# Attention and entropy layers on one core: next image's projection begins at the end of attention, in four PSUM banks, with three value banks ahead of the entropy steps

## The reference

```python
x = x + attention(_gn(x), w1, b1, a1, w2, b2, a2, wa, ba, aa)
#   q = prelu(w1 x + b1), k = prelu(w2 x + b2)   24 channels each
#   v = prelu(wa x + ba)                         192 channels
#   out = softmax(q^T k) v                       4096 x 4096 scores for each image
x = x + likelihood(_gn(x), m0..m3, b0..b3, f0..f2)
#   for lower = x - 0.5 and upper = x + 0.5, in each channel: four small layers 1 -> 3 -> 3 -> 3 -> 1,
#   logits = softplus(m) logits + b, and after the first three: logits += tanh(f) tanh(logits)
#   likelihood = max(|sigmoid(s upper) - sigmoid(s lower)|, 1e-6)
```

## Time and profile before

| | |
|---|---|
| median of 3 runs | 4902.97 us (4902.42 to 4907.78) |
| the profiled execution's own time | 4911.56 us |
| its span in the trace | 4909.8 us |
| busy: PE, DVE, ACT, POOL | 91%, 86%, 73%, 15% |

### The profile page before, as it was taken

The page is one execution under the profiler, slowest core; times in us unless marked ns, Lnnn a source line. Parts: engine busy times, 40 slices in busy tenths (PEclk is TensorE's granted clock), DMA queues, the critical chain, the costliest instruction groups (busy, mean ns, idle before and its releaser), DMA issues.

```text
span 4909.8 us, 106055 instructions
## 1 busy us (share of the span) xinstructions
PE 4460.9 (91%) x38328; PEld 2970.3 (60%) x38328; DVE 4209.1 (86%) x5569; ACT 3600.0 (73%) x3958; POOL 726.6 (15%) x769
## 2 busy tenths in 40 slices
PE   6999889998899988999899998999989998899976
PEld 4887338873488724787258862688616785178831
DVE  6997799978999789997899968999699996989866
ACT  2666887668767697676977669776697776966788
POOL 4200300003010130101300022000220103101012
PEclk9999999999999999999999999999999999999998
DMA  3001431014301142011520024210241113420133
GB/s 78 14 17 32 109 84 30 23 41 114 81 23 32 35 119 73 23 31 42 124 61 27 28 60 117 49 34 21 69 113 47 31 30 74 104 51 23 34 86 95
DMA packets 154987, 279.93 MB, mean 57 GB/s; under 512 B 37441, under 2 KB 37921, under 8 KB 152706
## 3 DMA queue, kind: packets, MB, share of 16 engines
q1 hardware_dynamic: 154434, 272.69, 21.6%
HBM read 205.24 MB, written 50.33 MB: 52 GB/s over the span
## 4 chain that ended last, share of the span: by engine, by line
PE 56%; DVE 16%; ACT 12%; issue 12%; DMA 1%; SPq 1%; DVEq 0%; POOL 0%; ACTq 0%; POOLq 0%
PE ps L1345 10%; PE ps L1347 10%; PE ps L1349 10%; PE ps L1121 7%; ACT th L669 6%; PE ps L1297 6%; DVE mxp L1026 5%; ACT arena L662 4%; DVE arena L922 3%; DVE th L960 3%; PE ps L1218 2%; PE ps L1204 2%; PE ps L1165 2%; PE ps L1176 2%; PE ps L1146 2%
## 5 line engine op out<-in xcount | busy, mean ns | idle before, releaser
L1345 PE MATMUL ps<-v_sb,arena 128*128 128x193 f16 x8192 | 2016.0, 246 | 14.7 <-DVE arena L922 14.7
L1347 PE MATMUL ps<-v_sb,arena 128*128 128x192 f16 x8192 | 2024.9, 247 | 0.0
L1349 PE MATMUL ps<-v_sb,arena 128*128 128x193 f16 x8192 | 2007.8, 245 | 0.0
L626 ACT ACTIVATE arena<-ps 128x1024 f16<-128x1024 f32 x1024 | 1050.5, 1026 | 896.3 <-PE ps L1121 896.2
L922 DVE TENSOR_TENSOR arena<-arena 128x1024 f16<-128x1024 f32 x1024 | 1293.6, 1264 | 213.7 <-ACT arena L629 213.6
L1026 DVE TENSOR_REDUCE mxp<-ps 128x1 f32<-128x512 f32 x1792 | 1177.9, 686 | 50.1 <-PE ps L1297 40.4
L960 DVE SCALAR_TENSOR_TENSOR th<-th,gates,ps 128x1024 f32<-128x1024 f32 x768 | 950.7, 1275 | 206.0 <-ACT th L669 201.0
L629 ACT ACTIVATE arena<-ps 128x1024 f32<-128x1024 f32 x1024 | 1045.6, 1021 | 0.2 <-DVE arena L922 0.2
L1347 PEld LDWEIGHTS ps<-v_sb,arena 128*128 128x128 f16 x8192 | 794.4, 97 | 262.4
L669 ACT ACTIVATE th<-ps,biases 128x1024 f32<-128x1024 f32 x768 | 827.0, 1118 | 114.1 <-PE ps L1204 77.8
L1345 PEld LDWEIGHTS ps<-v_sb,arena 128*128 128x128 f16 x8192 | 791.3, 97 | 143.6 <-issue 26.2
(11 more groups left out here) (120 smaller groups left out, 3189.7 us busy)
## 6 DMA issues: line engine op xcount, KB each, us to landing
x<-x2d SPq DMA_DIRECT2D x1152, 64.0 KB, 2.2
arena<-x2d SPq DMA_DIRECT2D x768, 64.0 KB, 2.4
xp<-x_dram SPq DMA_DIRECT2D x18, 1536.0 KB, 12.9
shared<-x_dram SPq DMA_DIRECT2D x64, 384.0 KB, 3.7
x2d<-shared SPq DMA_DIRECT2D x64, 384.0 KB, 3.0
res<-x2d SPq DMA_DIRECT2D x96, 256.0 KB
out_dram<-res SPq DMA_DIRECT2D x96, 256.0 KB
kst<-shared SPq DMA_DIRECT2D x32, 256.0 KB, 4.3
```

What stands on the lines that cost most here:

```text
L626: act.activation(e_hi[:, q % 4, :].rearrange("p (k n) -> p k n", k=2), sc, ACT.Exp)
L1345: pe.matmul(acc, eh, v_sb[:, m, 0:C + 1], start=(m == 0 and t % 2 == 0), stop=False, skip_group_check=True)
L1347: pe.matmul(acc[:, 0:C], eh, v_sb[:, m, VW:VW + C], start=False, stop=False, skip_group_check=True)
L1349: ins = pe.matmul(acc, el, v_sb[:, m, 0:C + 1], start=False, stop=(m == MT - 1), skip_group_check=True)
```

## The change

- `project(0)`, the next image's first query and key bank, moves on PE from the beginning of `phase_a` to the end of `phase_b`, behind the last block's matmuls. This is ahead of the loop's branch. Its ACT and DVE parts now come ahead of `add_half`, and `low_part(0)` moves behind the third piece of `chain2`.
- The query and key banks go round four PSUM banks (`n % 4`), and the waits of PE change with them (`bank_user`).
- `V_LEAD` falls from 6 to 3: the value banks in the entropy steps are in steps 0 to 12 in place of 0 to 9.
- The first maximum moves from step 11 to step 14 (`FIRST_AT`). Steps 14 to 38 hold 31 of them and step 39 the last: one in a step, two in steps 15, 19, 23, 27, 31 and 35. The split and the turn come one step earlier.

```diff
-V_LEAD = 6
+V_LEAD = 3
-FIRST_AT = 11
+FIRST_AT = VB - V_LEAD + 1
+TURN_AT = 43
+def first_maxima(s):
+    begin = sum(2 if k % 4 == 3 else 1 for k in range(FIRST_AT, s))
+    return list(range(begin, min(begin + (2 if s % 4 == 3 else 1), MAXES))) if s >= FIRST_AT else []
+def bank_of(n):
+    return n % 4 if n < QK else n % 2
+def bank_user(n):
+    return max(n - 3, 0) if n < QK + 2 else n - 1
...
 # POOL
                     queries(0)
+                    queries(1)
                 root2(l)
                 if proj:
-                    for n in range(1, QK):
+                    for n in range(2, QK):
...
 # DVE
                 denominators(l, BLOCKS - 1)
+                if proj:
+                    value(0)
                 add_half(l, BLOCKS - 1, 0)
                 add_half(l, BLOCKS - 1, 1)
...
                 next(chain2)
                 if proj:
-                    query(0)
-                next(chain2)
+                    value(1)
                 next(chain2)
                 next(chain2)
                 if proj:
-                    query(1)
+                    low_part(0)
+                next(chain2)
                 next(chain2)
...
-                        m = s - FIRST_AT
-                        if 0 <= m < MAXES:
+                        for m in first_maxima(s):
...
 # PE
+            def project(n):
+                for h in range(2):
+                    k = HALF + h
+                    ins = pe.matmul(ps[:, bank_of(n), :], w_s[0:k, h, 0:P], xp[0:k, h, n * N:(n + 1) * N],
+                                    start=(h == 0), stop=(h == 1))
+                ins.then_inc(proj_mm, 1)
...
                 def bank_free(n):
-                    if n >= 2:
-                        pe.wait_ge(val_ready, pj(BANKS, n - 1))
+                    if bank_user(n):
+                        pe.wait_ge(val_ready, pj(BANKS, bank_user(n)))
...
                 if proj:
-                    qk_bank(0)
                     qk_bank(1)
                 averages2(l, 0)
...
-                    if proj and 0 <= s - FIRST_AT < MAXES:
-                        first_max(s - FIRST_AT)
+                    if proj:
+                        for m in first_maxima(s):
+                            first_max(m)
...
 # PE, end of phase_b
+                pe.wait_ge(full_ready, pairs + PAIRS)
+                project(0)
```

More of the change, by code:

```diff
@@ L649, in negative @@
                         act.wait_ge(val_ready, pj(BANKS, n - 1))
-                    act.activation(p_neg[:, n % 2, 0:w], ps[:, n % 2, 0:w], ACT.Relu, scale=-1.0
+                    act.activation(p_neg[:, n % 2, 0:w], ps[:, bank_of(n), 0:w], ACT.Relu, scale=-1.0
                                    ).then_inc(neg_ready, 1)
@@ L936, in value @@
                     dve.scalar_tensor_tensor(p_val[:, n % 2, 0:w], p_neg[:, n % 2, 0:w], omac[:, col:col + 1],
-                                             ps[:, n % 2, 0:w], ALU.mult, ALU.add).then_inc(val_ready, 1)
+                                             ps[:, bank_of(n), 0:w], ALU.mult, ALU.add).then_inc(val_ready, 1)
                 def low_part(n):
@@ L1017, in phase_a @@
                                               ALU.max).then_inc(max_red, 1)
-                        if m == MAXES:
+                        if s == TURN_AT - 1:
                             split_max(pj(BLOCKS, 0), pj(BLOCKS * MAXES, 0))
-                        if m == MAXES + 1:
-                            rows_out(pj(BLOCKS, 0), 0, l is None)
+                        if s == TURN_AT:
+                            rows_out(pj(BLOCKS, 0), 0, False)
             def phase_b(b, l):
@@ L1159, in qk_bank @@
                         pe.wait_ge(ws_ready, pj(1, 1))
-                        if l is not None:
-                            pe.wait_ge(full_ready, l * BLOCKS * PAIRS + BLOCKS * PAIRS)
                     bank_free(n)
-                    for h in range(2):
-                        k = HALF + h
-                        ins = pe.matmul(ps[:, n % 2, :], w_s[0:k, h, 0:P], xp[0:k, h, n * N:(n + 1) * N],
-                                        start=(h == 0), stop=(h == 1))
-                    ins.then_inc(proj_mm, 1)
+                    project(n)
                 def value_bank(v):
@@ L1175, in value_bank @@
                             k = HALF + h
-                            ins = pe.matmul(ps[:, n % 2, i * C:(i + 1) * C], xp[0:k, h, m * P:(m + 1) * P],
+                            ins = pe.matmul(ps[:, bank_of(n), i * C:(i + 1) * C], xp[0:k, h, m * P:(m + 1) * P],
                                             w_s[0:k, h, P:PW], start=(h == 0), stop=(h == 1))
@@ L1282, in phase_a @@
                             second_layer(s - 1)
-                        if proj and s == FIRST_AT + MAXES + 1:
+                        if proj and s == TURN_AT:
                             turn_max(pj(BLOCKS, 0), 0)
```

## The result

The changed kernel took 5031.99 us in the median of 4 runs (5025.67 to 5040.27), against 4905.38 us (4902.42 to 4909.45) for the kernel before on the same chip: a ratio of 1.026 (95% interval 1.0248 to 1.0272). It is slower by 126.6 us, 18 us for each of the seven images whose `phase_a` carries the projection. The forecast was 4993 with a range up to 5022. The sign was right and so was the chain of waits behind the largest term; the time lies above the range.

The account below looks back on a forecast made before the run. PE, DVE and ACT are busy most of the time; ACT's chain through PE and DVE paces the entropy steps. Terms -6.2 + 1.2 + 2.3 + 16.2 - 0.6 = 12.9 us an image, 90 for seven: 4993 us, range 4922 to 5022.

Parts of the forecast that it names:

- The double steps: Steps with two maxima, 15 to 35: waits for DVE's reductions hold `second_layer` and delay ACT, +16.2 us an image.
- The change-over: From one image's attention to the next's first step: earlier norm and fewer value banks ahead, -6.2 us an image in sum.
- Bank 0 and the branch: At the loop's end, two matmuls queued ahead of PE's branch cost 0.3 us an image, bounds nothing to 1.7-2.7.
- The rival in which the bank delays the branch until both matmuls are through: At the loop's end, `turn_out` starts 1.7 us later in six images, 5001 us in all; chance 0.05.
- The first maximum: Step 14: the wait for the last value bank moves here from step 11 and delays ACT, +2.3 us an image.
- The moved value banks: Steps 10 to 12: ACT has one more `negative` in each, about 0.4 us apiece, +1.2 us an image.
- The end of the steps: Steps 40 to 42: no maximum on PE any more where ACT waits for PE, -0.6 us an image.
- faster: Entropy steps: the maxima's waits end in time ACT doesn't need, leaving -3.3 us an image, 4880 us; chance 0.10.

Follow-up runs that it names:

- fill: The changed kernel with the first maximum of each two-maxima step issued eight times and `first_layer` of the step behind it twice, same results: 4984.49 us.
- second_behind: The changed kernel with only the second maximum of each two-maxima step put after `second_layer` on PE: 4968.25 us.
- before_behind: The kernel before the change with its first maxima moved after second and third layer of their step, nothing else: 4897.65 us.
- head_alone: The changed kernel with six value banks ahead of the steps again and one maximum in a step from step 11: 4895.44 us.
- behind: The changed kernel with every maximum issued after `second_layer` and `third_layer` of its step on PE, nothing else: 4872.63 us.

## Why the prediction was right in kind and short in size

- **The step that failed is "The double steps", the term of +16.2 us an image.** It measured +21.3. Its chain (reduction, maximum, `second_layer`, tanh, gate, reduction) is right: at full clock `fill` measures 15.9 in steps 15 to 39. The missing part is that the term and its bound above (20 us, every double at 3.4) priced `second_layer` at 1.09 us throughout, while PE, idle in the very waits that the term counts, falls to half its clock and takes up to 1.99. That is 5.5 us an image (21.3 - 15.9), 38 us in all. The other terms together came out 1.8 us an image lower than predicted, partly by a wrong sign, and that hid 13 us of the miss. On the spans the prediction is short by 25 us (90 against 115.4). The forecast is short by 39, because it took off the 8.6 us by which the profiled execution of before stood over its median, while that of after stands 5 us under its own. With no slower PE in any bound, the range ended too low.
- **The change-over**, -6.5 without bank 0's 0.3, measured -6.8, from -5.4 to -8.6 in single images. Split: up to DVE's scaling of the weights (L872) 12.99 to 11.45, 1.5 where 1.9 was predicted; from there to h1(0) 21.10 to 15.80, 5.3 where 4.6 was. In the fourth image `first_layer(0)` stands 26.6 us behind the start of L1132 (2329.96 to 2356.53), where some 25.5 was named.
- **Bank 0 and the branch.** Between the end of attention's last matmul and `turn_out` there are 3.43 us in the mean of images 2 to 7, and 3.33 before: 0.1 where 0.3 was taken. The rival in which the bank delays the branch until both matmuls are through falls. In the traces the branch begins a fixed time before the end of attention's last matmul at all six jumps, 1.54 us before the change and 1.21 after it; the prediction took some 1 us, from the median of 4.56, while the jump ahead of the fourth image took 4.88. So bank 0 does put the branch off, by the 0.3 us that was priced, and the jumps then came out 0.2 us shorter in the mean. The source view of the changed kernel has the branch at

```profile
L1390 PEldq COMPARE_BRANCH  x7: 83/4192/4722, 1090.3 to 4802.7; - x7
```

  4.19 us in the median against 4.56 in the earlier trace rows, so the bank's matmuls are queued ahead of it and run while it is under way: L1147 ends at 2326.07 + 1.91 = 2327.98, and PE then idles 1.98 us.
- **The first maximum**, +2.3, measured +3.2. The wait was 2.53 us where 2.4 was named. The sum that gave 2.6 was right and the 0.3 taken off it was not: the times that it starts from already hold that wait. Where the clock stays full, step 14 lasts 7.62 us (`second_behind`, third to seventh image), 2.6 more than the 5.02 of before. The slow clock adds 0.6 in the mean. In the fourth image it adds 1.1, 0.9 of it from L1238 at 1.99 in place of 1.09 us.
- **The moved value banks**, +1.2, measured -1.0: the wrong sign. Before, these steps held the wait of 2.92 us at step 11, and the slow clock behind it (6.8 us of half clock in steps 10 to 14). The prediction counted 0.24 us for that wait as it stood in one place and nothing for the matmuls behind it. In the trace of before, L1218 took 1.99 us behind it:

```profile
2362.68 1.99 PE L1218 MATMUL ps<-th,w 64*64 64x512 f32 x8
```

  The 1.2 for the `negative`s doesn't show either: `before_behind` has no value bank in steps 10 to 12 and no maximum ahead of `second_layer`, and takes 17.19 us in steps 10 to 13, the changed kernel 17.11.
- **The end of the steps**, -0.6, measured -0.7, but that is luck. Steps 40 to 42, where the maxima are gone, give 0.2. The rest is step 44, 2.99 to 2.16 us, less 0.25 in step 45. In `head_alone`, where the turn of the maxima keeps its old step, step 44 takes 3.12, so the likely cause is the turn that comes one step earlier, which the prediction left at nothing.
- The rival "faster" is what `behind` does, and only because there `second_layer`, which ACT needs, isn't queued behind a maximum of its step. For maxima that hold nothing the prediction had about -4 us an image in one place and -3.3 in another; `behind` is at -5.9 an image.

## What to carry to other kernels

Where an engine works in program order, put a step that waits on a late result behind those that others wait for: the same doubles cost 21.3 us an image ahead of `second_layer`, and 0.4 behind it (1.6 against `before_behind`, whose single maxima stand behind it as well). Here the waits on PE cost twice, once as the wait and once as the slower matmuls behind it; to price one, take the duration of a matmul that stands behind a wait of the same length, not the usual one. And when a stall doesn't move with its suspected cause, look at what else has its last piece in that step: here it was two operations on an engine that is 15% busy.

## What the hardware showed that was not expected

- Waits of 1.0 to 2.6 us on PE, in two of every four steps, went with a granted clock at its lower level (1.2 GHz) for a part of the time: 0.88 over steps 15 to 39 of the fourth image, and 0.75 around step 19, against 0.98 over steps 15 to 39 of `behind`. With the waits partly filled, in `fill`, it stayed at 1.00. A group of eight matmuls then took up to 1.99 us in place of 1.09.
- More work made it faster. `fill` gives PE 85 more records in that stretch (618 from 533), and the kernel is 47.5 us faster than the changed one.
- The time of the jump at the end of PE's loop isn't fixed: 4.19 us in the median with two more matmuls queued ahead of it, 4.56 without, with nearly the same gap on the array (3.43 and 3.33 us). The medians of the other kernels divide in the same way: 3.93 to 4.44 us in the nine that have these matmuls there, 4.48 to 4.59 in the three that don't. Why is open.
